# Scatter with addition into three arrays in place of seven private rows per token

## What is computed

```python
scores = jax.nn.sigmoid(logits)                       # [T, 32 experts]
_, topidx = jax.lax.top_k(masked, TOP_K)              # 6 experts per token
tw = tw / (tw.sum(-1, keepdims=True) + 1e-20) * ROUTED_SCALE
eo = jnp.einsum('tei,eih->teh', jax.nn.silu(g) * u, w_down)
routed = jnp.einsum('te,teh->th', cw, eo)             # sum of 6 experts per token
lg = topidx[:, 0] // (E // L)
anchor = jnp.einsum('tl,tlh->th', acw, ao)            # 1 of 16 anchors per token
out = routed + shared + ANCHOR_ALPHA * anchor
```

## Time and profile before

| what | value |
|---|---|
| median of 3 runs | 397.11 us (394.73 to 398.8) |
| the profiled execution's own time | 397.25 us |
| its span in the trace | 395.5 us |
| PE, PEld, DVE, ACT, POOL busy | 334.6, 295.4, 264.9, 166.9, 188.6 us |
| routing and attention stages | until about 188 us |
| expert loop | about 188 to 358 us |
| last loads and additions, stores | about 358 to 395.5 us |

### The profile page before, as it was taken

One profiled execution on the slowest core, in us unless ns is written; L12 is line 12 of the kernel. 1 busy time (PEld: TensorE's weight loads), 2 busy tenths in 40 slices (PEclk: granted clock), 3 DMA queues, 4 the chain that ended last, 5 costly groups with the idle time before them and its releaser, 6 DMA issues.

```text
span 395.5 us, 8092 instructions
## 1 busy us (share of the span) xinstructions
PE 334.6 (85%) x2534; PEld 295.4 (75%) x2534; DVE 264.9 (67%) x1098; ACT 166.9 (42%) x431; POOL 188.6 (48%) x206
## 2 busy tenths in 40 slices
PE   5999999989999896878899999999999999990000
PEld 3786887958769684766798999999999999990000
DVE  3466688968979888488566755565555555654774
ACT  1133153253352533240377543436777777760000
POOL 5000000372672736614777777777766666663000
PEclk9999999989999998599999999999999999996555
DMA  7899997231269422359888877767766678624997
GB/s 228 248 358 332 310 425 307 59 116 60 86 193 383 155 74 86 115 209 402 271 245 250 246 214 215 205 202 221 210 208 196 190 227 286 186 103 151 277 282 229
DMA packets 42011, 86.61 MB, mean 219 GB/s; under 512 B 6785, under 2 KB 30905, under 8 KB 41705
## 3 DMA queue, kind: packets, MB, share of 16 engines
q1 hardware_dynamic: 32032, 59.84, 49.7%
q0 software_dynamic: 9072, 25.51, 18.1%
q10 hardware_dynamic: 864, 0.73, 0.7%
HBM read 50.71 MB, written 35.35 MB: 218 GB/s over the span
## 4 chain that ended last, share of the span: by engine, by line
PE 64%; DVE 13%; DMA 12%; ACT 4%; SPq 3%; issue 2%; POOL 0%; DVEq 0%; POOLq 0%; ACTq 0%
PE B L822 21%; PE B L840 11%; PE B L513 7%; PE B L803 6%; DMA W<-sums_d 5%; PE B L548 4%; DMA e_sb<-rows_d 3%; PE B L631 3%; PE B L617 2%; SPq L434 2%; PE B L597 2%; PE B L655 2%; DMA rows_d<-spent,slot 1%; DMA W<-in_pt 1%; DVE stats L1038 1%
## 5 line engine op out<-in xcount | busy, mean ns | idle before, releaser
L476 POOL DMA_INDIRECT rows_d<-spent,slot x77 | 74.6, 969 | 124.7 <-DVE slot L1248 103.1
L1492 DVE TENSOR_TENSOR e_sb<-e_sb,B 128x128 f32<-128x128 f32 (+1 forms) x112 | 32.2, 288 | 64.8 <-ACT e_sb L993 64.0
L497 POOL DMA_INDIRECT sums_d<-spent,to_row x60 | 58.1, 969 | 24.6 <-DVE spent L1484 15.1
L840 PE MATMUL B<-W,e_sb 128*128 (+1 forms) x224 | 67.1, 381 | 0.3 <-DVE e_sb L1492 0.3
L822 PEld LDWEIGHTS B<-e_sb,UPW 128*128 128x128 f32 x476 | 62.9, 191 | 4.3 <-issue 0.6
L822 PE MATMUL B<-e_sb,UPW 128*128 128x128 f32 x476 | 63.6, 275 | 0.3 <-ACT e_sb L988 0.3
L497 POOL DMA_INDIRECT sums_d<-Y_own,to_row x52 | 50.8, 977 | 21.0 <-DVE Y_own L1484 12.2
L993 ACT ACTIVATE e_sb<-B 128x128 f32<-128x128 f32 (+1 forms) x112 | 30.8, 275 | 46.5 <-PE B L822 45.2
L822 PEld LDWEIGHTS B<-e_sb,W 128*128 128x128 f32 x320 | 43.1, 191 | 2.8 <-ACT e_sb L988 0.5
L822 PE MATMUL B<-e_sb,W 128*128 128x128 f32 x320 | 43.6, 275 | 0.2 <-ACT e_sb L988 0.2
L803 PE MATMUL B<-ident,e_sb 128*128 128x128 f32 x224 | 42.7, 273 | 0.7 <-DMA e_sb<-rows_d 0.7
(11 more groups left out here) (182 smaller groups left out, 498.7 us busy)
## 6 DMA issues: line engine op xcount, KB each, us to landing
e_sb<-rows_d SPq DMA_DIRECT2D x112, 161.0 KB, 2.6
rows_d<-spent SPq DMA_DIRECT2D x1, 7728.0 KB, 33.4
W<-in_wx SPq DMA_DIRECT2D x1, 6643.0 KB, 48.4
W<-sums_d SPq DMA_DIRECT2D x13, 448.0 KB, 10.4
W<-in_wx SPq DMA_DIRECT2D x10, 516.5 KB, 8.6
W<-in_wx SPq DMA_DIRECT2D x1, 4576.0 KB, 16.9
W<-in_pt SPq DMA_DIRECT2D x4, 666.0 KB, 7.1
W<-sums_d SPq DMA_DIRECT2D x7, 336.0 KB, 12.2
```

The costliest lines, as they stand in the source:

```text
L476: pool.indirect_dma_start(rows_d, bass.IndirectOffsetOnAxis(ap=slot[0:n, t, j:j + 1], axis=0), xrow[0:n, t, :], None).then_inc(done, 16)
L497: pool.indirect_dma_start(sums_d, bass.IndirectOffsetOnAxis(ap=to_row[:, i:i + 1], axis=0), result(i), None).then_inc(y_sent[i % NY], 16)
L840: pe.matmul(B[6 + i % 2][:, 0:D], hid[:, i % 2, :], weights, start=True, stop=True).then_inc(D_ps, 1)
L1492: dve.tensor_tensor(out[0:n, i % 2, :], S[0:n, i % 2, :], ups, ALU.mult).then_inc(H_ok, 1)
```

## The change

Three arrays of 11 rows per partition take the place of the seven rows per token. Step i scatters to array i % 3, and the DMA adds to what is there (`compute_op=ALU.add`). Two DMAs that add to one array must not overlap, so from the fourth step on GpSimd also waits until the scatter of step i - 3 has landed. The arrays are filled with zeros at the start. A row in a list carries one number, the token's, and is 290 numbers long, not 322; DVE adds the array's offset when it takes the number out. The two routines that made 32 row numbers are gone, and so are the second pad row and `dummy_col`. The three arrays are loaded at the end, none inside the loop, and there are three rounds of additions, not seven.

```diff
-TO_ROW = EXPERTS + 1
-ROW = ALPHA_COL + 1 + TO_ROW
+ID_COL = ALPHA_COL + 1
+ROW = ID_COL + 1
-OWN_ROWS = CHOICES * NT
-SPARE_ROW = TP * OWN_ROWS + 8
+ARRAYS = 3
+OWN_ROWS = ARRAYS * NT
+SPARE_ROW = TP * OWN_ROWS
...
-PIECES = [[(0, 4), (4, 8), (8, NT)]] * (CHOICES - 1) + [[(0, 4), (4, 7), (7, 9), (9, 10), (10, NT)]]
+PIECES = [[(0, 4), (4, 8), (8, NT)]] * (ARRAYS - 1) + [[(0, 4), (4, 7), (7, 9), (9, 10), (10, NT)]]
...
-        sums_d = nc.dram_tensor("sums_d", [DUMMY_SPARE + 2 * TO_ROW * P, D], F32).ap()
+        sums_d = nc.dram_tensor("sums_d", [(TP + P) * OWN_ROWS, D], F32).ap()
...
-            for half, row in enumerate((padrow, pad_two)):
-                sp.dma_start(rows_d[DUMMY_ROW + half * P:DUMMY_ROW + (half + 1) * P, :], row[:, :]).then_inc(ini_d, 16)
-            of_choice = sums_d[1:1 + TP * OWN_ROWS, :].rearrange("(p c t) d -> p c t d", c=CHOICES, t=NT)
-            n = TILES[-1]
-            sp.dma_start(of_choice[n:TP, :, NT - 1, :], padrow[n:TP, 0:D].unsqueeze(1).to_broadcast([TP - n, CHOICES, D])).then_inc(ini_d, 16)
-            sp.dma_start(of_choice[TT:TP, :, 0:NT - 1, :].rearrange("p c t d -> p c (t d)"),
-                         h[TT:TP, 0:NT - 1, :].rearrange("p t d -> p (t d)").unsqueeze(1)
-                         .to_broadcast([TP - TT, CHOICES, (NT - 1) * D])).then_inc(ini_d, 16)
+            sp.dma_start(rows_d[DUMMY_ROW:DUMMY_ROW + P, :], padrow[:, :]).then_inc(ini_d, 16)
+            of_array = sums_d.rearrange("(p c t) d -> p c t d", c=ARRAYS, t=NT)
+            sp.dma_start(sums_d[0:SPARE_ROW, :].rearrange("(p r) d -> p r d", r=OWN_ROWS),
+                         padrow[0:TP, 0:D].unsqueeze(1).to_broadcast([TP, OWN_ROWS, D])).then_inc(ini_d, 16)
+            sp.dma_start(of_array[TP:TP + P, :, 0, :],
+                         padrow[:, 0:D].unsqueeze(1).to_broadcast([P, ARRAYS, D])).then_inc(ini_d, 16)
...
             for i in range(XT):
                 load_rows(i)
-                if i == XT - 16:
-                    for u in range(NY):
-                        sp.wait_ge(y_sent[u], 16 * sends_of(u, FIRST_ROUTED))
-                    load_part(TOPK)
             sp.wait_ge(D_ps, XT)
             for u in range(NY):
                 sp.wait_ge(y_sent[u], 16 * sends_of(u, XT))
-            for c in range(TOPK):
-                load_part(c)
+            for c in range(ARRAYS):
+                for q, (lo, hi) in enumerate(PIECES[c]):
+                    sp.dma_start(parts[:, c, lo:hi, :], of_array[0:TP, c, lo:hi, :]).then_inc(fin_ld[c][q], 16)
...
             for i in range(XT):
                 pool.wait_ge(Y_by[weighed_by_act(i)], weighed_before(i) + 1)
+                if i >= ARRAYS:
+                    pool.wait_ge(y_sent[(i - ARRAYS) % NY], 16 * ((i - ARRAYS) // NY + 1))
                 pool.indirect_dma_start(sums_d, bass.IndirectOffsetOnAxis(ap=to_row[:, i:i + 1], axis=0),
-                                        result(i), None).then_inc(y_sent[i % NY], 16)
+                                        result(i), None, compute_op=ALU.add).then_inc(y_sent[i % NY], 16)
...
-                order_choices(b)
...
-                choice_rows(b)
...
                 if looked_up(i):
-                    dve.tensor_copy(to_row[:, i:i + 1], to).then_inc(meta_ok, 1)
+                    dve.tensor_scalar(to_row[:, i:i + 1], of_token, float(i % ARRAYS * NT), None, ALU.add).then_inc(meta_ok, 1)
...
-            for c in range(CHOICES):
+            for c in range(ARRAYS):
                 for q, (lo, hi) in enumerate(PIECES[c]):
                     dve.wait_ge(fin_ld[c][q], 16)
                     m = dve.tensor_tensor(h[0:TP, lo:hi, :], h[0:TP, lo:hi, :], parts[:, c, lo:hi, :], ALU.add)
```

More of the change, by code:

```diff
@@ L108 @@
 TRI4 = 5 * LISTS
-SLOT_ADD = TRI4 + 16 + 6
-SMALL = SLOT_ADD + 8 * NT + 2
+SLOT_ADD = TRI4 + 16 + 5
+SPARE_PLUS = SLOT_ADD + 8 * NT + 2
+SMALL = SPARE_PLUS + LISTS
 SENT = [TP] * (NT - 1) + [-(-TILES[-1] // 16) * 16]
-TRASH_ROW = DUMMY_ROW + 2 * P
-DUMMY_SPARE = SPARE_ROW + LISTS * P
-PIECES = [[(0, 4), (4, 8), (8, NT)]] * (CHOICES - 1) + [[(0, 4), (4, 7), (7, 9), (9, 10), (10, NT)]]
-assert FIRST_ROUTED < XT and MORE <= 2 * TO_ROW
+TRASH_ROW = DUMMY_ROW + P
+PIECES = [[(0, 4), (4, 8), (8, NT)]] * (ARRAYS - 1) + [[(0, 4), (4, 7), (7, 9), (9, 10), (10, NT)]]
+assert FIRST_ROUTED < XT and MORE <= P
 LATE_PIECES = 10
@@ L209, in build @@
         iota_a, base0, tri4 = small[:, LISTS:LISTS + ANCHORS], small[:, 4 * LISTS:5 * LISTS], small[:, TRI4:TRI4 + 16]
-        number, row_of_number, dummy_row, dummy_col, first_w, pcol = (small[:, TRI4 + 16 + q:TRI4 + 17 + q]
-                                                                       for q in range(6))
+        number, row_of_number, dummy_row, first_w, pcol = (small[:, TRI4 + 16 + q:TRI4 + 17 + q] for q in range(5))
+        spare_plus = small[:, SPARE_PLUS:SPARE_PLUS + LISTS]
         Y_own = sb("Y_own", [P, NY_OWN * D])
@@ L215, in build @@
         h = sb("h", [P, NT, D])
-        token_row = sb("token_row", [P, 2, NT], I32)
-        to_rows = sb("to_rows", [P, NT])
+        token_row = sb("token_row", [P, NT + 1], I32)
         e_sb = sb("e_sb", [P, 2 * HEADS * TT])
@@ L269, in build @@
         UPW = sb("UPW", [P, 2, UP_COLS])
-        pad_two, pad_ids = UPW[:, 0, 0:ROW], UPW[:, 1, 0:2 * TO_ROW].bitcast(I32)
         wcol = sb("wcol", [P, XT])
         to_row = sb("to_row", [P, XT], I32)
-        parts = W[0:TP, 0:CHOICES * NT * D].rearrange("p (c t d) -> p c t d", c=CHOICES, t=NT)
+        parts = W[0:TP, 0:ARRAYS * NT * D].rearrange("p (c t d) -> p c t d", c=ARRAYS, t=NT)
         B = [ctx.enter_context(nc.psum_tensor(f"B{i}", [P, 512], F32)) for i in range(8)]
         rows_d = nc.dram_tensor("rows_d", [TRASH_ROW + P, ROW], F32).ap()
-        sums_d = nc.dram_tensor("sums_d", [DUMMY_SPARE + 2 * TO_ROW * P, D], F32).ap()
+        sums_d = nc.dram_tensor("sums_d", [(TP + P) * OWN_ROWS, D], F32).ap()
         ld = {n: sem(f"ld_{n}") for n in ["first", "gates", "consts", "rest", "lists", "late0", "late1"] +
@@ L307, in build @@
         y_sent = [sem(f"y_sent{u}") for u in range(NY)]
-        fin_ld = [[sem(f"fin_ld{c}_{q}") for q in range(len(PIECES[c]))] for c in range(CHOICES)]
+        fin_ld = [[sem(f"fin_ld{c}_{q}") for q in range(len(PIECES[c]))] for c in range(ARRAYS)]
         fin_ok, out_st = sem("fin_ok"), sem("out_st")
@@ L409, in _ @@
             sp.wait_ge(scat_anchor, 16 * NT)
-            sp.wait_ge(ini_d, 16 * 4)
+            sp.wait_ge(ini_d, 16 * 3)
             sp.wait_ge(av_ps, NT)
@@ L422, in load_rows @@
                 if looked_up(i):
-                    row = entry(mybir.EngineType.SP, 1, i, DUMMY_ROW + P)
+                    row = entry(mybir.EngineType.SP, 1, i, DUMMY_ROW)
                     rows = rows_d[bass.ds(row, P), :]
@@ L455, in _ @@
             pool.memset(ones[:, :], 1.0).then_inc(ini, 1)
-            for row in (padrow, pad_two):
-                pool.memset(row[:, 0:ALPHA_COL + 1], 0.0)
-            pool.iota(pad_ids[:, :], pattern=[[P, 2 * TO_ROW]], base=DUMMY_SPARE, channel_multiplier=1)
+            pool.memset(padrow[:, 0:ID_COL], 0.0).then_inc(ini, 1)
             pool.memset(xrow[:, :, ALPHA_COL:ALPHA_COL + 1], ANCHOR_ALPHA)
-            pool.iota(token_row[:, 0, :], pattern=[[1, NT]], base=1 - NT, channel_multiplier=OWN_ROWS)
-            pool.iota(token_row[:, 1, :], pattern=[[1, NT]], base=1 + TOPK * NT, channel_multiplier=OWN_ROWS).then_inc(ids_ok, 1)
+            pool.iota(token_row[:, 0:NT], pattern=[[1, NT]], base=0, channel_multiplier=OWN_ROWS)
+            pool.iota(token_row[:, NT:NT + 1], pattern=[[1, 1]], base=SPARE_ROW, channel_multiplier=OWN_ROWS).then_inc(ids_ok, 1)
             pool.wait_ge(ids_ok, 1)
[L463 to L466, removed]
+            pool.tensor_copy(padrow[:, ID_COL:ROW], token_row[:, NT:NT + 1]).then_inc(ini, 1)
+            pool.tensor_copy(xrow[:, :, ID_COL], token_row[:, 0:NT]).then_inc(ini, 1)
             pool.memset(h[:, :, :], 0.0).then_inc(ini, 1)
@@ L492, in _ @@
                 scatter(t, range(2 if t == NT - 3 else 1, CHOICES), scat)
[L494 removed]
+            pool.wait_ge(ini_d, 16 * 3)
             for i in range(XT):
                 pool.wait_ge(Y_by[weighed_by_act(i)], weighed_before(i) + 1)
+                if i >= ARRAYS:
+                    pool.wait_ge(y_sent[(i - ARRAYS) % NY], 16 * ((i - ARRAYS) // NY + 1))
                 pool.indirect_dma_start(sums_d, bass.IndirectOffsetOnAxis(ap=to_row[:, i:i + 1], axis=0),
[L498 removed]
+                                        result(i), None, compute_op=ALU.add).then_inc(y_sent[i % NY], 16)
         @block.tensor
@@ L1157, in weights @@
                                   ALU.mult).then_inc(ch_done, 1)
[L1159 to L1170, removed]
             def choose(b):
@@ L1363, in _ @@
             dve.memset(top_slots[:, :, :], 0.0)
-            for lo, hi in ((0, ALPHA_COL), (ALPHA_COL + 1, ROW - 1)):
-                dve.memset(xrow[96:P, 0:NT - 1, lo:hi], 0.0)
```

(17 more changed lines are left out.)

9 lines of the change are left out of this document (3 added, 6 removed).

## The result

The changed kernel takes 440.28 us (median of 4, 439.22 to 441.2) where the kernel before takes 396.83 (4 runs): the ratio is 1.111, with a 95% interval of 1.107 to 1.116. It is 43 us slower, and 56 us above the forecast of 384.

What follows compares the result with a forecast made beforehand. PE was taken to bound the expert loop and DMA loads the end, with GpSimd just catching up. The sum was 397.25 - 13.45 (end) - 0.45 (loop load) - 0.35 (row numbers) + 1.0 (landing) = 384.0 us, range 381 to 404.

Steps and rivals of the forecast that it cites:

- What bounds the kernel: Whole kernel: PE bounds the expert loop, DMA the end at 4.48 us a part; GpSimd has time to catch up.
- 1.376 us per interval: GpSimd's result scatters: 111 intervals between 205.35 and 358.10, the pace it can afford without delaying the end.
- GpSimd needs longer to make such a DMA: Rival at GpSimd's result scatters: 0.15 us more for 128 rows, interval 1.42, time 389 (388 to 401); chance 9%.
- x: Result scatters: extra time to landing because an addition reads the old row first; taken as 1.0 us, bounds 0 and 2.3.
- the forecast's 57%: Chance of the main case: the second wait in the loop costs 0 to 4 us, time 381 to 389, centre 384.
- the landing rival: Second wait, all 112 steps: additions land too late, GpSimd becomes the bound; 389 to 398 (12%) or 398 to 427 (22%).
- my rule for the interval: Second wait: the interval is a third of the time to landing, if that is more than 1.27 us.
- The 0.35 us that I had worked out: Alternative value of x, from the scatter queue's 0.34 us per scatter in the loop; it would give 383.4.
- The end: After the last scatter: three parts loaded, not six, at 4.48 us each; 13.45 us less.
- The load inside the loop: Step 96: SP's 22 waits and three loads go, and with them PE's two turns 1.93 us apart; 0.45 us less.
- row numbers: Choices of the blocks: scans and products removed; only the fifth block's choice gains, 0.35 us less.
- The zeros: SP's queue early on: 3.8 MB and 0.4 MB written, 15 us under 31 us of cover; price zero.

Runs made afterwards that it cites:

- e5: The changed kernel with each result scatter sending and adding only 64 of its 128 rows; 422.34 us.
- e6: The changed kernel with plain writes of 64 of the 128 rows in place of additions; 379.57 us.
- e4: The changed kernel with six arrays in place of three, each scatter waiting for the sixth one back; 451.39 us.
- e2: The kernel before, with its seven private rows per token, zeros in all of `sums_d` and adding scatters, none waiting for another; 461.05 us, ratio 1.164.
- e3: The changed kernel with two arrays in place of three, each scatter waiting for the second one back; 496.1 us.
- e1: The changed kernel with plain writes in place of additions, the second wait kept; 386.5 us, ratio 0.975 to the kernel before.
- e7: The changed kernel adding 128 rows of half the width (512 bytes); 436.63 us.
- e9: The kernel before with weighed results, `sums_d` and the parts in bfloat16, on 112 partitions; 387.74 us, ratio 0.976.

## Why the prediction was wrong

*What bounds the kernel* was read rightly. GpSimd's 1.376 us per interval was named as the number on which all depends, and on that the kernel failed: it needs 1.85. The sum's own interval had a floor of 1.27, a plain scatter's, so it held the addition's price on GpSimd at nothing.

*The step that failed* is the rival "GpSimd needs longer to make such a DMA". It stood with 9% and a price of 0.15 us, because I took the slope of the earlier trace rows (0.91, 0.94 and 0.97 us for 80, 112 and 128 rows) and doubled it. The slope part was right: e5 and e6 give 0.14 us for 128 rows. What the sizes of plain scatters can't show is a fixed cost of the addition: 0.44 us. Together 0.58, and the interval of 1.85 lies beyond the 1.5 from which I had called the gain gone. By my own sum, 205.35 + 111 x 1.85 = 410.7, and the range would have had to reach 437. I bounded this unknown from one side only: as with x, a plain instruction's whole time once more (0.97) was the row from above, and I left it out. The sign that the prediction had named for this rival (a scatter of over 1.1 us) did come, 1.55 us; its last sentence, that nothing but x reaches 5 us, was wrong.

*The landing.* x was 0.9 to 1.6 where I took 1.0, in the mean a little more; but most of it is GpSimd's longer instruction, which I had priced apart. Less that, the DMA itself takes 0.3 to 1.0 us longer. In e4 and e2, with more in flight, the landings are longer and the interval is the same. So the forecast's 57% and the landing rival's 34% argued about a term that cost 4.3 us. It did cost these, in part by a 0.75 us restart that I did not have.

*A second error, hidden by the first.* Without the restart my rule for the interval gave too little wherever the wait binds, and in my own sum it bound until 250. An estimate, from the prediction's landings (x = 1.0) and the 0.75 of e3 and e1: intervals of 1.92, 1.68 and 1.52 us, so 10 scatters by 225, 15 more by 250, and the last at about 380, 22 us behind PE; the time is then some 406 us, slower than before even with a scatter of 0.97 us. No run has an adding scatter that is that short, so this stays an estimate.

*DMA as the limit.* Its share rose from 0.68 to 0.90 in the loop, while the bytes fell from 205 to 153 GB/s, as feared; e7 shows that it decides nothing here. The 0.35 us that I had worked out from the Trainium skill ("Collectives: The Full Stack", the bandwidth ceiling: two sources on one read ring, half the rate, which the page states for ReduceScatter) were too few for the queue. Its share per scatter went from 0.34 us to 59.5% x 70 / 38 = 1.10 us of all engines, three times, not twice.

*The end*: 13.45 us less forecast; from the last scatter to the end of the span it is 37.4 - 24.7 = 12.7 less, although the landing is 1.0 longer, so 13.7 for the rest. Right.

*The load inside the loop, row numbers*: the 0.45 us can't be seen under GpSimd's pace. In e1, where PE sets the pace again, no two turns of PE are over 1.6 us apart, so the 1.93 of the earlier trace rows is gone, as said. The first scatter starts 2.9 us earlier than before, but in the changed kernel and in e1 and e3 to e7 it starts anywhere from 202.4 to 206.0 with the same code ahead of it, so the 0.35 us for the removed scans are neither shown nor refuted.

*The zeros*: free, as said (73.7 against 113.38 us); e2 shows a price once the cover is gone, 10 us for 24 MB.

*The whole without the addition*: e1's 386.5 us against the 383 that the same sum gives without x. The 3.5 us are GpSimd's delay by the second wait (3.3 of them): with plain landings of 2.8 us, (2.8 + 0.75) / 3 is 1.18, under 1.27, but the long ones (up to 4.9) bind one by one and are not won back.

## What to carry to other kernels

An operation that no trace shows needs a bound on the engine that issues it as well as on the engine that does it, and the slope over sizes of another operation says nothing about its fixed part. Where a queue issues a hundred of them, compare the interval it can afford (here 1.376 us) with the instruction's own time before anything else; one run with the operation switched on and all else left alone gives it. A wait that binds costs its restart as well as the landing (here 0.75 us). And a stage bound by loads should be asked first at what rate it loads: 112 partitions gave 282 GB/s where 128 gave 403.

## What the runs showed of the hardware that was not expected

- An indirect DMA of 128 rows of 1 KB that adds in DRAM holds GpSimd for 1.547 us, a plain one for 0.969; 64 rows 1.403 and 0.895. The width of a row (512 or 1024 bytes) doesn't enter.
- The adding scatters' queue moved some 140 packets each (5331 for 38 in 70 us), the plain ones 47 (2464 for 52), for the same 128 rows, with three times the share of DMA's time.
- After a landing on which GpSimd really waits it mostly starts the next DMA 0.73 to 0.75 us later (e1, e3); where the landing came earlier the gap is 0.30.
- Loads of 4 KB rows into 112 partitions ran at 282 GB/s, into 128 partitions at 403.
- DVE's additions of 112x1024 took as long with one operand in bfloat16 as with both in float32 (1.22 us, e9 and the kernel before).
